# The exponential of the whole decay sum, taken from a third matmul to a product on GpSimd

## The reference, cut to what matters

```
A_cumsum = jnp.cumsum(A, axis=-1)                                   # inside a chunk
decay_states = jnp.exp(A_cumsum[:, :, :, -1:] - A_cumsum)           # from a position to the chunk's end
states = jnp.einsum('bclhn,bhcl,bclhp->bchpn', Bm, decay_states, X)
decay_chunk = jnp.exp(segsum(A_last))                               # A_last: the whole sum of a chunk
new_states = jnp.einsum('bhzc,bchpn->bzhpn', decay_chunk, states)
state_decay_out = jnp.exp(A_cumsum)                                 # from the chunk's start to a position
```

## Time and profile before

| | us |
|---|---|
| median of 3 runs | 2229.65 |
| lowest, highest | 2222.31, 2231.4 |
| the profiled execution, its own time | 2230.16 |
| its span, first to last instruction | 2228.3 |

### The profile page before, as it was taken

One profiled execution on the slowest core, in us unless ns is written; L12 is line 12 of the kernel. 1 busy time (PEld: TensorE's weight loads), 2 busy tenths in 40 slices (PEclk: granted clock), 3 DMA queues, 4 the chain that ended last, 5 costly groups with the idle time before them and its releaser, 6 DMA issues.

```text
span 2228.3 us, 65452 instructions
## 1 busy us (share of the span) xinstructions
PE 1744.2 (78%) x25602; PEld 1397.1 (63%) x25602; DVE 1616.2 (73%) x5205; ACT 1108.5 (50%) x2124; POOL 1278.5 (57%) x1346
## 2 busy tenths in 40 slices
PE   3566610009999994899999999999999936999997
PEld 2445510007777773788878777877788724777775
DVE  3877883206777776578898989898989864777775
ACT  2223300007777774565555555545554315777775
POOL 2210147764787776344546565656666664777776
PEclk9767765559999997899999999999999857999998
DMA  9200001315555554400000000000000014555553
GB/s 146 72 23 2 25 18 37 128 54 160 181 182 187 190 191 100 60 4 3 3 3 11 11 10 11 11 11 10 10 10 12 12 39 163 189 182 192 185 184 107
DMA packets 95635, 174.31 MB, mean 78 GB/s; under 512 B 53602, under 2 KB 66939, under 8 KB 95348
## 3 DMA queue, kind: packets, MB, share of 16 engines
q10 hardware_dynamic: 21312, 102.00, 13.8%
q1 hardware_dynamic: 56372, 42.14, 8.3%
q0 software_dynamic: 17664, 26.27, 3.5%
HBM read 134.99 MB, written 37.31 MB: 77 GB/s over the span
## 4 chain that ended last, share of the span: by engine, by line
PE 53%; DVE 22%; issue 11%; POOL 8%; ACT 4%; DMA 1%; SPq 1%; DVEq 0%; ACTq 0%; POOLq 0%
PE ps L1026 10%; PE ps L1027 9%; PE ps L1028 9%; PE ps L1118 6%; POOL rows L632 6%; PE ps L1153 3%; PE ps L1167 2%; PE ps L1076 2%; PE ps L996 2%; PE ps L1189 1%; PE ps L1048 1%; ACT rounded L870 1%; PE ps L1164 1%; PE ps L1172 1%; PE ps L1121 1%
## 5 line engine op out<-in xcount | busy, mean ns | idle before, releaser
L1026 PE MATMUL ps<-rounded 97*128 97x512 f32 (+2 forms) x952 | 394.0, 414 | 4.5 <-DVE rounded L1770 2.8
L1027 PE MATMUL ps<-rounded 97*128 97x512 f32 (+2 forms) x952 | 377.0, 396 | 0.0
L1028 PE MATMUL ps<-rounded 97*128 97x512 f32 (+2 forms) x952 | 376.4, 395 | 0.0
L1118 PE MATMUL ps<-rounded 128*128 128x224 f32 (+1 forms) x2256 | 353.6, 299 | 4.4 <-ACT rounded L870 4.4
L848 ACT ACTIVATE rounded<-ps 128x512 fp32r<-128x512 f32 x444 | 267.2, 602 | 162.2 <-PE ps L1028 154.7
L1118 PEld LDWEIGHTS ps<-rounded 128*128 128x128 f32 x2256 | 307.9, 200 | 38.7 <-issue 8.8
L1805 DVE TENSOR_TENSOR rounded<-arena,rounded 128x512 fp32r<-128x512 f32 x296 | 222.0, 750 | 136.2 <-ACT arena L849 136.0
L664 POOL TENSOR_TENSOR rounded<-arena,rounded 128x512 fp32r<-128x512 f32 x148 | 192.7, 1302 | 160.9 <-ACT arena L849 157.9
L849 ACT ACTIVATE arena<-ps 128x512 f32<-128x512 f32 x444 | 267.1, 602 | 0.0
L710 POOL TENSOR_TENSOR w<-arena,consts 128x384 f32<-128x384 f32 x128 | 107.7, 841 | 219.8 <-DVE arena L1327 219.8
L1026 PEld LDWEIGHTS ps<-rounded 97*128 97x128 f32 (+2 forms) x952 | 166.7, 175 | 57.8 <-issue 10.4
(11 more groups left out here) (309 smaller groups left out, 3816.0 us busy)
## 6 DMA issues: line engine op xcount, KB each, us to landing
rounded<-weights_by_expert ACTq DMA_DIRECT2D x148, 673.0 KB, 4.6
arena<-rows SPq DMA_DIRECT2D x74, 208.0 KB, 2.7
residual<-in_x SPq DMA_DIRECT2D x16, 384.0 KB, 7.1
weights_by_expert<-rounded SPq DMA_DIRECT2D x8, 672.0 KB, 3.2
residual<-after_ffn SPq DMA_DIRECT2D x12, 384.0 KB, 6.8
rows<-xn SPq DMA_DIRECT2D x17, 208.0 KB, 8.3
after_ffn<-arena POOLq DMA_INDIRECT x148
out<-arena POOLq DMA_INDIRECT x148
```

The source lines that it names most:

```text
L1026: pe.matmul(dst, left[0], right[0], start=start, stop=False)
L1027: pe.matmul(dst, left[1], right[0], start=False, stop=False)
L1028: return pe.matmul(dst, left[0], right[1], start=False, stop=stop)
L1118: pe.matmul(dst[:, 0:w], x3[:, x_part, n, slot, tokens], wtap[:, w_part, n, y + 1, 0:w], start=(y == 0 and n == x_part == w_part == 0), st ...
```

## The change

`sums` keeps two matmuls. `decays` takes the exponential of two thirds, 96 columns. POOL forms the third one from the two, 128 x 48 elements, right behind `xw`, and counts it on its chain. `decayed` waits for that chain in the place of ACT's exponentials.

```
             def decayed(g, i):
                 pool.wait_ge(s["state"], g * SIDE + (i + 1))
                 if i % Q == 0:
-                    pool.wait_ge(s["ex"], g * NQ + (i // Q + 1))
+                    ch.wait()
                 pool.tensor_tensor(st1[:, :, :], st[:, :, :],
                                    ex3[:, i // Q % 2, 2, i % Q, :].unsqueeze(2).to_broadcast([P, NH, HD]), ALU.mult).then_inc(s["s1"], 1)
...
                     pool.wait_ge(s["ex"], c + 1)
                     ch.link(pool.tensor_tensor(wdt[:, :, :], dt[:, c % 2, :, :], ex3[:, c % 2, 1, :, :], ALU.mult))
                     scaled(c, xw, wdt[:, :, :], "xw")
+                    ch.done(pool.tensor_tensor(ex3[:, c % 2, 2, :, :], ex3[:, c % 2, 0, :, :], ex3[:, c % 2, 1, :, :], ALU.mult))
...
-                act.activation(ex3[:, c % 2, :, :, :].rearrange("p a b c -> p (a b c)"), bank(7)[:, 0:3 * Q * NH], ACT.Exp).then_inc(s["ex"], 1)
+                act.activation(ex3[:, c % 2, 0:2, :, :].rearrange("p a b c -> p (a b c)"), bank(7)[:, 0:2 * Q * NH], ACT.Exp).then_inc(s["ex"], 1)
...
-                for n, w in enumerate((upto, later, whole)):
+                for n, w in enumerate((upto, later)):
                     ins = pe.matmul(bank(7)[:, n * Q * NH:(n + 1) * Q * NH], w, a, start=True, stop=True)
```

## The result

| the session of the prediction | median us | lowest, highest | runs |
|---|---|---|---|
| kernel before | 2228.36 | 2222.06, 2233.09 | 9 |
| changed kernel | 2238.81 | 2228.95, 2243.52 | 9 |

The changed kernel was slower: ratio 1.0044, 95% interval 1.0023 to 1.0066. The forecast was 2226 us with a range up to 2236, so it missed, in size and in direction. The mean of the three ratios at 2230 us is 1.0020. There are two questions: where the 4.5 us of the forecast went, and what the loss is.

What follows compares the result with a forecast made beforehand. PE alone was taken to set the pace from 950 to 1070 us, then partly DVE. From 2230.2 us, minus 4.5 (shorter `sums`) plus 0.8 (DVE held by POOL) gave 2226.5, predicted as 2226 us; range 2217 to 2236.

Steps and rivals of the forecast that it cites:

- the 4.5 us of the forecast: Second mixer, PE's `sums`: gain from dropping the third matmul, a third of 13.4 us; bounds nothing and 7.3 us.
- the sum of the pieces: `sums` (L1137) has 18 chain pieces in 32 quads, 13.4 us; a third of each was taken as gain, 4.5 us.
- the 25.47 forecast: Where PE is full, 950 to 1070 us: `sums` would start 25.47 us apart, against 25.67 before.
- rival (2): No gain: PE's 0.2 us waited away at DVE's next product, or loads were hidden; 2229.5 to 2230.5 us, chance 0.13.
- in POOL's own order: POOL's queue behind `xw`: the product costs nothing thanks to room before its consumers; without that cover 9.1 us.
- Rival (4): Slower: DVE held in routing quads, PE waits longer before L1150, one more 1.7 us clock drop per unit; 2240 us, chance 0.13.
- the four or five named: Clock drops of the slower rival at which it sets in, given as the range's upper end, 2236 us.
- Rival (3): Faster: chain returns to PE in the other quads, or PE's clock drops less often; 2219 us, chance 0.19.
- the 0.8 us: DVE instructions ending with POOL's `xw`: eight on the chain, each held 0.1 us by the product; bounds nothing and 2.3 us.
- the moved wait: `decayed` (L722) waits for POOL's own chain instead of ACT; claimed to cost nothing.
- the upper bound: SBUF contention rule: DVE held for the full product, 0.286 us, at each of eight chain places; 2.3 us.
- the 0.28 us of room: Between POOL's L403 and ACT's L916 in one quad: just the product's price, so ACT may be late by 0.01 us.

Runs made afterwards that it cites:

- y3: The kernel before with POOL's 128 row scatters (L738) issued only after the mixer's last row; 2344.35 us, ratio 1.0294 to the kernel before.
- y4: The changed kernel with POOL's 128 row scatters (L738) issued only after the mixer's last row; 2343.68 us, ratio 1.0294 to the kernel before.
- after: Profile of the changed kernel in the session of the prediction, span 2236.9 us; that session's median 2238.81 us, ratio 1.0044.
- u2: The changed kernel, unchanged, timed and profiled again on a second chip; 2233.60 us, ratio 1.0006 to the kernel before.
- z2: The changed kernel, unchanged, timed and profiled again in a later session; 2236.39 us, ratio 1.0010 to the kernel before.
- z1: The changed kernel with POOL's product moved behind the normalisation (L403), to the end of POOL's step; 2232.68 us, ratio 1.0008 to the kernel before.
- z: Later session: the changed kernel again, and with its product moved behind L403, against the kernel before at 2232.11 us; ratios 1.0010 and 1.0008.
- u: Later session on a second chip: both kernels again, unchanged, against the kernel before at 2231.62 us; before 1.0003, changed 1.0006.
- x: Later session, kernel before at 2278.92 us: before again 1.0019, changed again 0.9958, PE and ACT part alone 0.9941, POOL part alone 1.0000.
- x1: The kernel before, unchanged, built and run once more on a slower chip; 2283.65 us, ratio 1.0019.
- x2: The changed kernel, unchanged, once more on a slower chip; 2271.90 us, ratio 0.9958 to the kernel before.
- y: Later session, kernel before at 2285.53 us: PE and ACT part 0.9958, POOL part 0.9983, both kernels with scatters after the last row 1.0294.

## Why the prediction was wrong

**The step that failed first is the sum of the pieces.** The forecast took a third of each of 18 pieces of the chain, 4.5 us. By place these are: the seven up to 1070 us, 5.5 us and a third 1.8; the eleven behind, 7.9 us and a third 2.6. The first part came: 25.49 us from quad to quad where PE is full, against the 25.47 forecast, and some 1.9 us in rows 0 to 35 at full clock. The second part did not come at all: from row 35 to 119 the pair y3 and y4 shows 0.2 us of difference in 569. A piece of the chain says what the end waited for as the kernel ran, not how far the next engine is behind. In y4 the pieces are nearly all still there and their 0.2 us each are waited away in between; in after, u2 and z2 most are gone, and the chain runs over DVE and POOL in their place. That is rival (2)'s mechanism, in two thirds of the mixer.

**The second step is that PE's other instructions were taken to last as long as before.** Two groups did not:

- In rows 119 to 127 the clock, +3.2 us, and in the same low clock the product behind them (2.03 against 3.73 us), part of the +2.0 us behind row 127. The rest there changes from profile to profile (z2 0.8 us over the mean of before, after 2.8). The clock of these rows is the one loss that stands in every profile of the changed kernel at 2230 us, and it is larger than the gain of the shorter matmuls in rows 0 to 35.
- Between rows 35 and 119 the scan runs met more scatters, 3.8 us more of holds in the mean, in three profiles of three. The prediction does not name L738's effect on PE at all; its sentence that the product costs nothing "in POOL's own order" looked for waits, and here there are none. What these holds cost is not shown: the rows are 2.2 us longer in the mean, but only by z2, and DVE may hide a hold of PE there as it hides the shorter matmul. Why the runs meet scatters more often is argued, not shown: the product moves the scatters against PE's runs, and shorter quads move the runs against the scatters; each half alone brings a part.

**Rival (4) was the right kind and had the wrong place.** It named fewer granted cycles as what would make the kernel slower, but put them into the eight routing units as more short drops. The window from 1070 to 1770 us is at 0.96 as before; it was one stretch at the end in which the clock no longer came back. (The range's upper end, 2236 us, is six such drops of 1.7 us above the forecast, not the four or five named.) Rival (3), the same thing as a gain, is seen too, in rows 0 to 35; it was given 0.19 against 0.13 with no row to rank them. Rival (2), no gain, is what rows 35 to 119 show, and its 0.13 was too little.

**The port and POOL's order.** No L1426 and no L1465 (longest 1453 ns, before 1452) grew by the product, and the three L1424 at 1126 us by 0.14 us (1.40, before 1.26), so the 0.8 us were too much; the moved wait shows no cost. The Trainium skill (SBUF — State Buffer, "Who interferes with whom") has the second of the two engines blocked until the first finishes; the 1480 ns agree with that for `xw` alone, since the next POOL instruction did not extend it. The prediction had put the upper bound by that rule, the product in full at each place; but the DVE instruction was issued before the product, and the rule gives it the turn. POOL's order used up the 0.28 us of room in front of ACT's L917. The prediction put that at 0.01 us; ACT now waits there in 8 quads, 1.8 us, and POOL stands on the chain in rows 35 to 119 for 42 to 85 us where it had nothing. In z1, where the product no longer stands in front, it has 8 us, and the time is the same, so no cost of it can be told.

**The size of the first session.** The profiles account for 4.5 us. The medians of that session differ by 10.4, those of z and u by 4.3 and 2.0. The time follows the mean granted clock: in z it was 0.8776 before and 0.8752 after, in u 0.8772 and 0.8763, in the first session 0.8751 after. In z's runs of the changed kernel 0.001 of clock goes with 1.7 us, in u's with 0.5. So the loss at 2230 us is a few us at most: z and u alone could not tell it from nothing, and the first session stood at its upper end. Whether by chance of nine runs or by its chip is not settled.

By the profiles, then, the forecast's -4.5 and +0.8 stand against: -2.7 (rows 0 to 35), +2.2 (rows 35 to 119), +3.2 (clock of the last rows) and +2.0 (behind them), which but for rounding is the 4.5 us by which the spans differ. Of these the +3.2 is in every profile; the -2.7 is in part the clock, and the +2.2 is z2's alone.

**What stays open.** Why the clock does not come back in the last rows is not known: both halves of the change delay it, and the profile shows no idle time of PE that is new there. Why the change came out faster in x, the one session at 2280 us with the whole change as it is, is open too. There the mean clock was the same or a little higher (session x: 0.8684 before, 0.8689 after), which fits the sign, but the profiled executions of x1 and x2 (spans 2285.9 and 2287.9) don't show the 0.4%, and the changed kernel has not fewer holds there but more (81 of 47.2 us against 72 of 40.5). What a scatter's issue and PE have in common was not tried. No version here beats the kernel before on both kinds of chip by more than can be told.

## What to carry to other kernels

The sum of an instruction's pieces on the chain of waits is not what shortening it is worth. Here the full piece counted only where the engine has no idle time over a whole stretch (up to 1070 us), and nothing where a second engine is nearly as busy. A gain of the forecast's size in one pair of profiles is no proof either: in y3 and y4 it was mostly the clock, and the granted clock of each stretch has to be compared first. Look besides for instructions whose duration varies though they wait for nothing (the scan run, 0.99 us mostly and up to 1.6 at full clock), and for stretches where the clock is in doubt, such as the last rows, and put the range there. A result within 0.5% wants both kernels again on another chip before its sign is believed: here the sign itself changed.

## What was not expected of the hardware

- An indirect transfer's issue on POOL holds PE inside a run of small matmuls that waits for nothing: some 0.2 us a time where the kernel before takes 2230 us, 0.5 to 0.7 where it takes 2280. With the scatters late, 3 scan runs are over 1.5 us long in either kernel, against 31 to 39 in the six other kernels of x and y (first weight load to last).
- Chips differ by 2% in this kernel: 2228 to 2232 us in four sessions, 2279 to 2286 in three, and most of the difference arises in the rows with scatters (row 35 to 119: 593 and 592 us against 626 and 631, and 569 with the scatters late on such a chip), the rest in the last rows and behind them.
- The clock at the mixer's end comes back alike over sessions where the kernel before takes 2230 us, in either kernel: the product behind row 127 takes 2.03 us in both profiles of before and 3.73 in all three of after. What looked like noise belongs to the kernel.
